# Cross attention on one core: nine batches instead of eight turned by VectorE, in groups of two and one, and ScalarE asking for the context's plain copies

## The chip, the cores and the metric

The kernel runs on one core of a Trainium2 chip. The metric is the device time of one execution in microseconds (us). Before the change the median of three runs was 129.13 us (129.09 to 129.58).

## What is computed

For each of 16 batches there are two inputs of 128 channels x 1024 positions, X (`x`) and G (`ctx_4096`), and eight 128x128 weights. Cut to what matters:

```python
def xca(q, k, v):                                   # 8 heads of 16 channels
    attn = softmax(einsum('bhni,bhnj->bhij', q, k) * scale, axis=-1)
    return einsum('bhnd,bhde->bhne', v, attn)       # back to [b, n, c]
res_p2r = xca(heads(rgb, wq_rgb), heads(geo, wk_point), heads(geo, wv_point)) @ proj_p2r.T
res_r2p = xca(heads(geo, wq_point), heads(rgb, wk_rgb), heads(rgb, wv_rgb)) @ proj_r2p.T
return transpose(rgb + res_p2r) + transpose(geo + res_r2p)
```

`rgb` is X and `geo` is G with channels last. The attention is over channels, so its scores are made of one 128x128 Gram matrix of X and G per batch, with the weights on both sides. For that Gram matrix (a sum over the 1024 positions) TensorE needs X and G with positions on the partitions, that is, turned.

## The kernel before, in words

The kernel is a hand-written pipeline over rounds. In round `i` the engines work on five batches at once: batch `i` is turned, batch `i-1` gets its Gram matrix (L291), batch `i-2` its products with the weights and its scores (uv, s), batch `i-3` its softmax and the two small products y (L342) and t (L355, L356), and batch `i-4` its output: twelve float32r matmuls of 512 columns from the plain copies (L312), split into a high and a low part. Round 16 is the last full one; a tail follows.

A batch can be turned in one of two ways.

- By TensorE (`on_tensor`): sixteen 128x128 transposes (L270) of the plain copies `x_raw`, `g_raw` into PSUM. ScalarE then copies X's half out (L438) and VectorE G's (L541).
- By VectorE (`on_vector`): four stream transposes of 32x32 blocks (L534) straight into `xt` and `gt`. They read `xz` and `gz`, a second copy of the batch, loaded by DMA in four parts of 32 partitions ("quads", L158), each with runs of 1 KB. A pair of batches fills one of two slots. The plain copy of the batch is loaded as well, for the output.

Before, the batches 5, 6, 8, 9, 11, 12, 14 and 15 are turned by VectorE.

All waits are written by hand on semaphores. Each engine runs its own list in order. These orders matter here:

- SyncE (its queue is SPq) asks in each round for plain copies of X and of G, 512 KB each, then for quads 0 and 1 of `xz` (X of a pair) or `gz` (G of a pair), then for a store. Before a plain copy into one of the six `x_raw`/`g_raw` slots it waits until GpSimd is done with the slot's last batch (`x_lo_ready`, `g_lo_ready`). Plain copies are asked for three rounds ahead of a batch that TensorE turns, one round ahead of one that VectorE turns.
- ScalarE (ACTq) asks for quads 2 and 3, one early and one late in its round, between its own copies.
- `issued_in` says in which round a pair is asked for: X in round 2, 4, then one round after the pair that used the slot before was turned; G one round after X. Before that `pair_turned` waits for the slot. The four quads of one tensor and pair add to one semaphore (`xz_loaded`, `gz_loaded`) and VectorE waits for all four.
- VectorE turns G's first half between the softmax's normalisation (L568) and its copy of y (L576), for which TensorE waits with the t product (L355).

Of the kernel before, what the change touches and what calls it, by code (L numbers as in the profile page):

```python
# [14 lines left out]
QUAD = 32  # L15
RAW_SLOTS = 6
SPLIT_SLOTS = 3
OUT_SLOTS = 5
PAIRS = 2
# [3 lines left out]
WQR, WKR, WKP, WQP, PP, PR, WVP, WVR = range(8)  # L23


VECTOR_PAIRS = ((5, 6), (8, 9), (11, 12), (14, 15))


def bass_cross_channel_attention(nc: bass.Bass, x, ctx, weights, out):
# [10 lines left out]
    B, C, N = x.shape  # L40
# [2 lines left out]
    HALF = N // 2  # L43
    TILES = N // TILE
    QUADS = P // QUAD
    on_vector = [b for pair in VECTOR_PAIRS for b in pair]
    on_tensor = [b for b in range(B) if b not in on_vector]
    assert C == P and HALF == BANK and B == 16 and on_tensor[0] == 0

    with ExitStack() as stack:  # L50
# [13 lines left out]
        x_raw = sb("x_raw", [P, RAW_SLOTS, N])  # L64
        g_raw = sb("g_raw", [P, RAW_SLOTS, N])
# [43 lines left out]
        x_loaded = [sem(f"x_loaded{s}") for s in range(RAW_SLOTS)]  # L109
        g_loaded = [sem(f"g_loaded{s}") for s in range(RAW_SLOTS)]  # L110
# [12 lines left out]
        xt_turned = sem("xt_turned")  # L123
        gt_ready = sem("gt_ready")
# [18 lines left out]
        x_lo_ready = sem("x_lo_ready")  # L143
        g_lo_ready = sem("g_lo_ready")
# [7 lines left out]

        def load_turned(eng, src, dst, loaded, pair, quads):

            first = VECTOR_PAIRS[pair][0]
            for q in quads:
                into = dst[q * QUAD:(q + 1) * QUAD, pair % PAIRS, :, :]
                eng.dma_start(into.rearrange("p e (a m) -> p (e a) m", a=QUADS),  # L158
                              src[q][:, QUADS * first:QUADS * (first + 2), :]).then_inc(loaded[pair % PAIRS], 16)

        def pair_turned(eng, pair):

            eng.wait_ge(xt_turned, 4 * pair + 4)
            eng.wait_ge(gt_ready, 2 * VECTOR_PAIRS[pair][1] + 2)

        def x_turned_half(eng, b, half):

# [2 lines left out]
            else:  # L170
                eng.wait_ge(xt_copied, 2 * on_tensor.index(b) + 1 + half)


        issued_in = {2 + 2 * pair if pair < PAIRS else VECTOR_PAIRS[pair - PAIRS][1] + 1: pair
                     for pair in range(len(VECTOR_PAIRS))}

        first, second = slice(0, HALF), slice(HALF, N)
        third, fourth = slice(HALF, HALF + HALF // 2), slice(HALF + HALF // 2, N)
# [31 lines left out]

        @block.sync
        def _(sp):
            def load_plain(b):
                slot = b % RAW_SLOTS
                sp.dma_start(x_raw[:, slot, :], x[b]).then_inc(x_loaded[slot], 16)
                sp.dma_start(g_raw[:, slot, :], ctx[b]).then_inc(g_loaded[slot], 16)

            def store(b):
                sp.wait_ge(half_copied, 2 * b + 2)
                sp.dma_start(out[b], out_sb[:, b % OUT_SLOTS, :]).then_inc(out_stored[b % OUT_SLOTS], 16)  # L220

            sp.dma_start(x_raw[:, 0, first], x[0][:, first]).then_inc(x_first, 16)
            sp.dma_start(x_raw[:, 0, second], x[0][:, second]).then_inc(x_loaded[0], 16)
            load_plain(1)
            sp.dma_start(w_sb[:, WQR:WKR + 1, :], weights[:, WQR:WKR + 1, :]).then_inc(wu_loaded, 16)
            load_plain(2)
            sp.dma_start(w_sb[:, WKP:, :], weights[:, WKP:, :]).then_inc(w_loaded, 16)
            load_plain(3)
            load_plain(4)

            for i in range(2, B + 4):
                for b in range(5, B):
                    if i == max(2, b - 1 if b in on_vector else b - 3):
                        if b >= RAW_SLOTS:
                            sp.wait_ge(x_lo_ready, b - RAW_SLOTS + 1)
                            sp.wait_ge(g_lo_ready, b - RAW_SLOTS + 1)
                        load_plain(b)
                x_pair, g_pair = issued_in.get(i), issued_in.get(i - 1)  # L240
                if x_pair is not None:
                    if x_pair >= PAIRS:
                        pair_turned(sp, x_pair - PAIRS)
                    load_turned(sp, x_turn, xz, xz_loaded, x_pair, (0, 1))
                if g_pair is not None:
                    load_turned(sp, g_turn, gz, gz_loaded, g_pair, (0, 1))
                if i >= 5:
                    store(i - 5)
            last_slot = (B - 1) % OUT_SLOTS
            sp.wait_ge(half_copied, 2 * B - 1)  # L250
            sp.dma_start(out[B - 1][:, first], out_sb[:, last_slot, first]).then_inc(last_stored[0], 16)
            sp.wait_ge(quarter_copied, 1)
            sp.dma_start(out[B - 1][:, third], out_sb[:, last_slot, third]).then_inc(last_stored[1], 16)
            sp.wait_ge(quarter_copied, 2)
            sp.dma_start(out[B - 1][:, fourth], out_sb[:, last_slot, fourth]).then_inc(last_stored[2], 16)
            for s in range(OUT_SLOTS):
                sp.wait_ge(out_stored[s], 16 * len(range(s, B - 1, OUT_SLOTS)))
            for part in range(3):
                sp.wait_ge(last_stored[part], 16)
# [157 lines left out]
        def _(act):  # L417
            def split_hi(b, raw, loaded, hi, hi_ready):
                plain_loaded(act, b, loaded)
                if b == 0:  # L420
                    act.wait_ge(x_first, 16)
                    act.wait_ge(g_first, 16)
                if b >= SPLIT_SLOTS:
                    act.wait_ge(half_done, 2 * (b - SPLIT_SLOTS) + 2)
                nc.scalar.copy(hi[:, b % SPLIT_SLOTS, :], raw[:, b % RAW_SLOTS, :]).then_inc(hi_ready, 1)  # L425

            def evacuate(b, half):
                act.wait_ge(half_done, 2 * b + 1 + half)
                if half == 0 and b >= OUT_SLOTS:
                    act.wait_ge(out_stored[b % OUT_SLOTS], 16 * (b // OUT_SLOTS))  # L430
                cols = slice(half * HALF, (half + 1) * HALF)
                nc.scalar.copy(out_sb[:, b % OUT_SLOTS, cols], out_ps[:, cols]).then_inc(half_copied, 1)  # L432
# [36 lines left out]
            for i in range(B + 1):  # L469
                s, y, l = i - 2, i - 3, i - 4  # L470
                x_pair, g_pair = issued_in.get(i), issued_in.get(i - 1)
                if s >= 0:
                    gram_high(s)
                if y >= 0:
                    exponents(y)
                if s >= 0:
                    split_hi(s, x_raw, x_loaded, x_hi, x_hi_ready)
                if x_pair is not None:
                    if x_pair >= PAIRS:
                        pair_turned(act, x_pair - PAIRS)  # L480
                    load_turned(act, x_turn, xz, xz_loaded, x_pair, (2,))
                if g_pair is not None:
                    load_turned(act, g_turn, gz, gz_loaded, g_pair, (2,))
                if l >= 0:
                    evacuate(l, 0)
                if l >= 0 and l != B - 4:
                    evacuate(l, 1)
                if s >= 0:
                    copy_uv(s)
                if i in on_tensor:  # L490
                    copy_xt(i, 0)
                if s >= 0:
                    split_hi(s, g_raw, g_loaded, g_hi, g_hi_ready)
                if x_pair is not None:
                    load_turned(act, x_turn, xz, xz_loaded, x_pair, (3,))
                if g_pair is not None:
                    load_turned(act, g_turn, gz, gz_loaded, g_pair, (3,))
                if i in on_tensor:
                    copy_xt(i, 1)
                if y >= 0:  # L500
                    t_high(y)
                if i == 1:
                    act.wait_ge(wu_loaded, 16)
                    nc.scalar.copy(wu_hi[:, :, :], w_sb[:, WQR:WKR + 1, :]).then_inc(wu_hi_ready, 1)
# [19 lines left out]
        @block.vector  # L524
        def _(dve):
            def turn_half(b, half, src, loaded, dst, turned):
                n = on_vector.index(b)
                pair, at = n // 2, n % 2
                dve.wait_ge(loaded[pair % PAIRS], 64 * (pair // PAIRS) + 64)
                dve.wait_ge(gram_done, b - 1)  # L530
                blocks = src[:, pair % PAIRS, at, :].rearrange("p (a j i) -> p j a i", a=QUADS, i=QUAD)
                first = half * TILES // 2
                cols = slice(half * HALF, (half + 1) * HALF)
                nc.vector.transpose(dst[:, b % 2, cols].rearrange("p (j a k) -> p j a k", a=QUADS, k=QUAD),  # L534
                                    blocks[:, first:first + TILES // 2, :, :]).then_inc(turned, 1)
# [119 lines left out]
```

## Time and profile before

| what | value |
|---|---|
| median of three runs | 129.13 us |
| profiled execution | 129.13 us, of which 127.1 us from its first to its last instruction |
| PE, ACT, POOL, DVE busy | 95%, 68%, 61%, 56% of the span |
| DMA moved | 34.25 MB, 270 GB/s over the span |
| x_raw, g_raw, median from issue to landing | 15.8 and 16.2 us |

PE is TensorE, ACT ScalarE, DVE VectorE, POOL GpSimd, SPq and ACTq the sequencers that issue DMAs. PEclk is the clock that TensorE was granted, in parts of full speed; it is 1.00 throughout. A time such as "at 63.8" is counted from the first instruction.

### The profile page before, as it was taken

The numbers are of one execution on the slowest core, as the hardware profiler recorded it, in microseconds if no ns is written. First come the engines' busy times: TensorE is split into PE (matmuls) and PEld (weight loads), VectorE is DVE, ScalarE is ACT, GpSimd is POOL, SyncE is SP. The second block draws the span as 40 slices with busy tenths as digits, with TensorE's granted clock in tenths as the row PEclk, the third lists the DMA queues.
The fourth block names the chain that finished last, engine by engine and source line by source line (L and its number), as shares of the span: only waits on it lengthen the run. The fifth ranks groups of instructions, "written<-read, shape, count | busy, mean of one in ns | idle before, by whom it ended". The sixth has DMA issues, their size and how long they took to land.

```text
span 127.1 us, 2678 instructions
## 1 busy us (share of the span) xinstructions
PE 120.8 (95%) x858; PEld 110.0 (87%) x858; DVE 71.4 (56%) x210; ACT 86.4 (68%) x195; POOL 77.3 (61%) x41
## 2 busy tenths in 40 slices
PE   6979999999999999999999999999999998997990
PEld 6859998899898989898989989999989897985880
DVE  0035364637878625969653787862596965546210
ACT  4133967875959595878787595959587868588351
POOL 5000779685495958195958559595819595937700
PEclk9999999999999999999999999999999999999999
DMA  3999999999999999999999999999999750003435
GB/s 102 362 398 409 419 285 252 230 289 256 296 243 251 246 328 370 328 271 281 313 274 339 380 328 282 278 280 300 329 418 419 317 233 1 0 23 147 168 142 191
DMA packets 16493, 34.25 MB, mean 270 GB/s; under 512 B 1376, under 2 KB 9952, under 8 KB 16480
## 3 DMA queue, kind: packets, MB, share of 16 engines
q1 hardware_dynamic: 11840, 29.36, 72.9%
q10 hardware_dynamic: 4640, 4.72, 14.4%
q8 instruction: 7, 0.11, 0.4%
q14 instruction: 6, 0.05, 0.1%
HBM read 25.69 MB, written 8.39 MB: 268 GB/s over the span
## 4 chain that ended last, share of the span: by engine, by line
PE 84%; DMA 5%; ACT 3%; issue 2%; DVE 1%; SPq 1%; ACTq 1%
PE out_ps L312 32%; PE gram_bank L291 21%; PE sy_bank L342 6%; DMA g_raw<-in_ctx_dram 5%; PE gt_ps L270 5%; PE xt_ps L270 4%; PE t_bank L355 3%; PE sy_bank L366 3%; PE sy_bank L365 3%; PE t_bank L356 3%; ACT expd L454 2%; PE uv_bank L333 1%; PE uv_bank L335 1%; PE uv_bank L334 1%; DVE probs L568 1%
## 5 line engine op out<-in xcount | busy, mean ns | idle before, releaser
L205 POOL TENSOR_TENSOR x_lo<-x_raw,x_hi 128x1024 fp32r<-128x1024 f32 x16 | 38.0, 2378 | 39.0 <-ACT x_hi L425 39.0
L208 POOL TENSOR_TENSOR g_lo<-g_raw,g_hi 128x1024 fp32r<-128x1024 f32 x16 | 38.0, 2373 | 2.5 <-ACT g_hi L425 2.5
L291 PE MATMUL gram_bank<-gt,xt 128*128 128x128 f32 x256 | 33.8, 275 | 0.0
L291 PEld LDWEIGHTS gram_bank<-gt,xt 128*128 128x128 f32 x256 | 31.2, 192 | 0.0
L541 DVE COPY gt<-gt_ps 128x512 f32<-128x512 f32 x16 | 11.0, 687 | 18.9 <-PE gt_ps L270 18.9
L432 ACT COPY out_sb<-out_ps 128x512 f32<-128x512 f32 x31 | 18.0, 581 | 5.2 <-PE out_ps L312 3.9
L454 ACT ACTIVATE expd<-scores,min_neg 128x128 f32<-128x128 f32 x32 | 12.6, 396 | 8.6 <-DVE min_neg L551 8.6
L425 ACT CAST g_hi<-g_raw 128x1024 fp32r<-128x1024 f32 x16 | 16.9, 1055 | 0.0
L425 ACT CAST x_hi<-x_raw 128x1024 fp32r<-128x1024 f32 x16 | 16.6, 1037 | 0.0
L438 ACT COPY xt<-xt_ps 128x512 f32<-128x512 f32 x16 | 9.4, 586 | 9.1 <-PE xt_ps L270 9.1
L312 PE MATMUL out_ps<-x_hi,t_hi 128*128 128x512 f32 x31 | 13.6, 440 | 0.0
L467 ACT CAST t_hi<-t_bank 128x256 fp32r<-128x256 f32 x16 | 5.9, 371 | 10.8 <-DVE t_bank L580 10.8
L312 PE MATMUL out_ps<-g_lo,t_hi 128*128 128x512 f32 x31 | 12.4, 402 | 0.0
L580 DVE TENSOR_TENSOR t_bank<-t_bank,ident 128x256 f32<-128x256 f32 x16 | 6.9, 432 | 9.6 <-PE t_bank L356 9.6
L312 PE MATMUL out_ps<-x_lo,t_hi 128*128 128x512 f32 x31 | 12.3, 397 | 0.0
L312 PE MATMUL out_ps<-g_hi,t_lo 128*128 128x512 f32 x31 | 12.2, 395 | 0.0
L312 PE MATMUL out_ps<-x_hi,t_lo 128*128 128x512 f32 x31 | 12.2, 395 | 0.0
L312 PE MATMUL out_ps<-g_hi,t_hi 128*128 128x512 f32 x31 | 12.2, 394 | 0.0
L576 DVE COPY y_sb<-sy_bank 128x256 f32<-128x256 f32 x16 | 6.8, 424 | 8.8 <-PE sy_bank L342 8.8
L534 DVE STREAM_TRANSPOSE gt<-gz 128x512 f32<-128x512 f32 x16 | 11.2, 702 | 0.0
L534 DVE STREAM_TRANSPOSE xt<-xz 128x512 f32<-128x512 f32 x16 | 11.0, 685 | 0.0
L342 PE MATMUL sy_bank<-w_sb,probs 128*128 128x128 f32 x64 | 9.9, 277 | 1.0 <-DVE probs L568 1.0
(80 smaller groups left out, 211.5 us busy)
## 6 DMA issues: line engine op xcount, KB each, us to landing
x_raw<-in_x_dram SPq DMA_DIRECT2D x15, 512.0 KB, 15.8
g_raw<-in_ctx_dram SPq DMA_DIRECT2D x15, 512.0 KB, 16.2
out_dram<-out_sb SPq DMA_DIRECT2D x15, 512.0 KB, 15.1
xz<-in_x_dram SPq DMA_DIRECT2D x8, 256.0 KB, 12.4
gz<-in_ctx_dram SPq DMA_DIRECT2D x8, 256.0 KB, 16.0
xz<-in_x_dram ACTq DMA_DIRECT2D x8, 256.0 KB, 11.8
gz<-in_ctx_dram ACTq DMA_DIRECT2D x8, 256.0 KB, 13.9
g_raw<-in_ctx_dram ACTq DMA_DIRECT2D x2, 256.0 KB, 4.6
```

The source lines that it names most:

```text
L205: nc.gpsimd.tensor_tensor(x_lo[:, slot, :], x_raw[:, raw_slot, :], x_hi[:, slot, :].bitcast(F32), ALU.subtract).then_inc(x_lo_ready, 1)
L208: nc.gpsimd.tensor_tensor(g_lo[:, slot, :], g_raw[:, raw_slot, :], g_hi[:, slot, :].bitcast(F32), ALU.subtract).then_inc(g_lo_ready, 1)
L270: last = nc.tensor.transpose(ps[:, t * TILE:(t + 1) * TILE], raw[:, b % RAW_SLOTS, cols], ident2[:, 0, :])
L291: last = nc.tensor.matmul(gram_ps, xt[:, b % 2, cols], gt[:, b % 2, cols], start=(t == 0), stop=(t == TILES - 1))
L312: last = nc.tensor.matmul(out_ps[:, cols], w[:, b % 2, which, :], moving[:, slot, cols], start=(n == 0), stop=(n == len(parts) - 1))
L342: last = nc.tensor.matmul(y_ps[:, a * P:(a + 1) * P], probs[:, a, :], w_sb[:, wv, :], start=True, stop=True)
L425: nc.scalar.copy(hi[:, b % SPLIT_SLOTS, :], raw[:, b % RAW_SLOTS, :]).then_inc(hi_ready, 1)
L432: nc.scalar.copy(out_sb[:, b % OUT_SLOTS, cols], out_ps[:, cols]).then_inc(half_copied, 1)
L438: nc.scalar.copy(xt[:, b % 2, half * HALF:(half + 1) * HALF], xt_ps[:, :]).then_inc(xt_copied, 1)
L454: nc.scalar.activation(expd[:, a, :], scores[:, a, :], ACT.Exp, bias=min_neg[:, a:a + 1], scale=-1.0, accum_out=row_sum[:, a:a + 1]).then_ ...
L534: nc.vector.transpose(dst[:, b % 2, cols].rearrange("p (j a k) -> p j a k", a=QUADS, k=QUAD), blocks[:, first:first + TILES // 2, :, :]).t ...
L541: nc.vector.tensor_copy(gt[:, b % 2, half * HALF:(half + 1) * HALF], gt_ps[:, :]).then_inc(gt_ready, 1)
```

## The change

VectorE turns nine batches: 5, 6, 8, 9, 10, 11, 13, 14 and 15, in the groups (5,6), (8,9), (10,11), (13,14) and (15). TensorE turns 0 to 4, 7 and 12. The slots for a group, the rounds in which it is asked for and its waits follow the same rule as before, so that group (10,11) is asked for in rounds 7 and 8, (13,14) in 10 and 11, and (15) in 12 and 13. From batch 5 on, the plain copies of G are asked for by ScalarE in the middle of its round, those of X by SyncE, each waiting only for the slot of its own tensor.

```diff
-VECTOR_PAIRS = ((5, 6), (8, 9), (11, 12), (14, 15))
+VECTOR_GROUPS = ((5, 6), (8, 9), (10, 11), (13, 14), (15,))
...
+            first, count = VECTOR_GROUPS[pair][0], len(VECTOR_GROUPS[pair])
             for q in quads:
-                into = dst[q * QUAD:(q + 1) * QUAD, pair % PAIRS, :, :]
+                into = dst[q * QUAD:(q + 1) * QUAD, pair % PAIRS, 0:count, :]
                 eng.dma_start(into.rearrange("p e (a m) -> p (e a) m", a=QUADS),
-                              src[q][:, QUADS * first:QUADS * (first + 2), :]).then_inc(loaded[pair % PAIRS], 16)
+                              src[q][:, QUADS * first:QUADS * (first + count), :]).then_inc(loaded[pair % PAIRS], 16)
...
-            eng.wait_ge(xt_turned, 4 * pair + 4)
-            eng.wait_ge(gt_ready, 2 * VECTOR_PAIRS[pair][1] + 2)
+            last = VECTOR_GROUPS[pair][-1]
+            eng.wait_ge(xt_turned, 2 * on_vector.index(last) + 2)
+            eng.wait_ge(gt_ready, 2 * last + 2)
...
+        def plain_issued_in(i):
+            return [b for b in range(5, B) if i == max(2, b - 1 if b in on_vector else b - 3)]
...
-        issued_in = {2 + 2 * pair if pair < PAIRS else VECTOR_PAIRS[pair - PAIRS][1] + 1: pair
-                     for pair in range(len(VECTOR_PAIRS))}
+        issued_in = {2 + 2 * pair if pair < PAIRS else VECTOR_GROUPS[pair - PAIRS][-1] + 1: pair
+                     for pair in range(len(VECTOR_GROUPS))}
...
+            def load_plain_x(b):
+                if b >= RAW_SLOTS:
+                    sp.wait_ge(x_lo_ready, b - RAW_SLOTS + 1)
+                sp.dma_start(x_raw[:, b % RAW_SLOTS, :], x[b]).then_inc(x_loaded[b % RAW_SLOTS], 16)
...
-                for b in range(5, B):
-                    if i == max(2, b - 1 if b in on_vector else b - 3):
-                        if b >= RAW_SLOTS:
-                            sp.wait_ge(x_lo_ready, b - RAW_SLOTS + 1)
-                            sp.wait_ge(g_lo_ready, b - RAW_SLOTS + 1)
-                        load_plain(b)
+                for b in plain_issued_in(i):
+                    load_plain_x(b)
...
+            def load_plain_g(b):
+                if b >= RAW_SLOTS:
+                    act.wait_ge(g_lo_ready, b - RAW_SLOTS + 1)
+                nc.scalar.dma_start(g_raw[:, b % RAW_SLOTS, :], ctx[b]).then_inc(g_loaded[b % RAW_SLOTS], 16)
...
                     split_hi(s, g_raw, g_loaded, g_hi, g_hi_ready)
+                for b in plain_issued_in(i):
+                    load_plain_g(b)
```

## Rows read from the trace of the kernel before

**Rows 1.** The page: busy shares, and the span in 40 equal slices.

```profile
PE 120.8 (95%) x858; PEld 110.0 (87%) x858; DVE 71.4 (56%) x210; ACT 86.4 (68%) x195; POOL 77.3 (61%) x41
...
DMA  3999999999999999999999999999999750003435
GB/s 102 362 398 409 419 285 252 230 289 256 296 243 251 246 328 370 328 271 281 313 274 339 380 328 282 278 280 300 329 418 419 317 233 1 0 23 147 168 142 191
```

**Rows 2.** The chain that ended last: start, us, what (rounds 9, 10, 13, 15).

```profile
57.78 2.81 PE out_ps L312 x12
...
62.28 0.22 PE t_bank L355 x2
...
64.06 2.81 PE out_ps L312 x12
...
67.23 0.44 PE xt_ps L270 x4
67.66 0.44 PE gt_ps L270 x4
...
72.10 2.81 PE out_ps L312 x12
...
84.66 2.81 PE out_ps L312 x12
...
98.97 2.81 PE out_ps L312 x12
```

**Rows 3.** Timeline of DVE in round 11: start, us, line, [idle before <-releaser].

```profile
73.99 0.70 DVE L534 STREAM_TRANSPOSE gt<-gz 128x512 f32<-128x512 f32 x1
74.61 0.67 DVE L534 STREAM_TRANSPOSE xt<-xz 128x512 f32<-128x512 f32 x1
75.74 0.42 DVE L576 COPY y_sb<-sy_bank 128x256 f32<-128x256 f32 x1 [0.45 <-PE sy_bank L342]
```

**Rows 4.** One issue of gz, the last ACTq one of batches 11, 12.

```profile
L158 ACTq DMA_DIRECT2D gz<-in_ctx_dram x1: 317/317/317, 54.8 to 54.8; - x1
...
DMA to landing us min/median/max: 17.0/17.0/17.0
```

**Rows 5.** The last SPq issue of gz, batches 14 and 15.

```profile
L158 SPq DMA_DIRECT2D gz<-in_ctx_dram x1: 2485/2485/2485, 77.1 to 77.1; - x1
...
DMA to landing us min/median/max: 16.3/16.3/16.3
```

**Rows 6.** Windows: stretch, its us, busy PE, PEld, DVE, ACT, POOL, PEclk, DMA, GB/s.

```profile
50.00:69.00 19.00, 19.00 (x133) 17.38 (x132) 13.36 (x39) 14.52 (x34) 12.87 (x6) 1.00 1.06 301
69.00:91.00 22.00, 22.00 (x160) 20.38 (x160) 14.21 (x41) 16.05 (x37) 15.26 (x7) 1.00 1.06 310
92.00:100.00 8.00, 8.00 (x56) 7.24 (x55) 6.73 (x22) 5.83 (x16) 4.97 (x3) 1.00 1.01 408
```

**Rows 7.** Timeline of SPq from 36 to 58 us.

```profile
44.37 0.33 SPq L215 DMA_DIRECT2D x_raw<-in_x_dram  x1
44.74 0.45 SPq L216 DMA_DIRECT2D g_raw<-in_ctx_dram  x1
...
52.41 4.69 SPq L158 DMA_DIRECT2D gz<-in_ctx_dram  x2
```

**Rows 8.** Waits of the SP queue: us in total, times, longest.

```profile
SPq L238 <- POOL g_lo L208: 13.4, 3, 7.6
```

**Rows 9.** Timeline of ACT in round 8, which issues two DMAs.

```profile
52.72 1.04 ACT L425 CAST x_hi<-x_raw 128x1024 fp32r<-128x1024 f32 x1
...
54.78 0.32 ACTq L158 DMA_DIRECT2D gz<-in_ctx_dram  x1
54.83 0.38 ACT L461 COPY uv<-uv_bank 128x256 f32<-128x256 f32 x1
```

**Rows 10.** Timeline: ACT in round 9 (no DMA), POOL's low part of batch 6.

```profile
59.00 1.03 ACT L425 CAST x_hi<-x_raw 128x1024 fp32r<-128x1024 f32 x1
...
56.23 2.38 POOL L208 TENSOR_TENSOR g_lo<-g_raw,g_hi 128x1024 fp32r<-128x1024 f32 x1
```

**Rows 11.** One ACTq issue of xz, ten us after ACTq's issue before it.

```profile
L158 ACTq DMA_DIRECT2D xz<-in_x_dram x1: 317/317/317, 64.8 to 64.8; - x1
...
DMA to landing us min/median/max: 9.0/9.0/9.0
```

More of the change, by code:

```diff
@@ L45, in bass_cross_channel_attention @@
     QUADS = P // QUAD
-    on_vector = [b for pair in VECTOR_PAIRS for b in pair]
+    on_vector = [b for group in VECTOR_GROUPS for b in group]
     on_tensor = [b for b in range(B) if b not in on_vector]
@@ L153, in load_turned @@
         def load_turned(eng, src, dst, loaded, pair, quads):
-            first = VECTOR_PAIRS[pair][0]
+            first, count = VECTOR_GROUPS[pair][0], len(VECTOR_GROUPS[pair])
             for q in quads:
-                into = dst[q * QUAD:(q + 1) * QUAD, pair % PAIRS, :, :]
+                into = dst[q * QUAD:(q + 1) * QUAD, pair % PAIRS, 0:count, :]
                 eng.dma_start(into.rearrange("p e (a m) -> p (e a) m", a=QUADS),
-                              src[q][:, QUADS * first:QUADS * (first + 2), :]).then_inc(loaded[pair % PAIRS], 16)
+                              src[q][:, QUADS * first:QUADS * (first + count), :]).then_inc(loaded[pair % PAIRS], 16)
         def pair_turned(eng, pair):
-            eng.wait_ge(xt_turned, 4 * pair + 4)
-            eng.wait_ge(gt_ready, 2 * VECTOR_PAIRS[pair][1] + 2)
+            last = VECTOR_GROUPS[pair][-1]
+            eng.wait_ge(xt_turned, 2 * on_vector.index(last) + 2)
+            eng.wait_ge(gt_ready, 2 * last + 2)
         def x_turned_half(eng, b, half):
@@ L212, in _ @@
         def _(sp):
+            def load_plain_x(b):
+                if b >= RAW_SLOTS:
+                    sp.wait_ge(x_lo_ready, b - RAW_SLOTS + 1)
+                sp.dma_start(x_raw[:, b % RAW_SLOTS, :], x[b]).then_inc(x_loaded[b % RAW_SLOTS], 16)
             def load_plain(b):
-                slot = b % RAW_SLOTS
-                sp.dma_start(x_raw[:, slot, :], x[b]).then_inc(x_loaded[slot], 16)
-                sp.dma_start(g_raw[:, slot, :], ctx[b]).then_inc(g_loaded[slot], 16)
+                load_plain_x(b)
+                sp.dma_start(g_raw[:, b, :], ctx[b]).then_inc(g_loaded[b], 16)
             def store(b):
@@ L233, in _ @@
             for i in range(2, B + 4):
-                for b in range(5, B):
-                    if i == max(2, b - 1 if b in on_vector else b - 3):
-                        if b >= RAW_SLOTS:
-                            sp.wait_ge(x_lo_ready, b - RAW_SLOTS + 1)
-                            sp.wait_ge(g_lo_ready, b - RAW_SLOTS + 1)
-                        load_plain(b)
+                for b in plain_issued_in(i):
+                    load_plain_x(b)
                 x_pair, g_pair = issued_in.get(i), issued_in.get(i - 1)
@@ L526, in turn_half @@
             def turn_half(b, half, src, loaded, dst, turned):
-                n = on_vector.index(b)
-                pair, at = n // 2, n % 2
+                pair = [b in group for group in VECTOR_GROUPS].index(True)
+                at = VECTOR_GROUPS[pair].index(b)
                 dve.wait_ge(loaded[pair % PAIRS], 64 * (pair // PAIRS) + 64)
```

## The prediction

> **What bounds the kernel now.** I read the page first. TensorE is busy 95% of the span, and in the line of slices the DMA engines stand at 9 as well until about slice 31, some 102 us, after which they are almost idle [rows 1]. So two things run full at once: TensorE, and until 102 us the DMA engines. Next I read the chain of work that ended last. Rounds start with the twelve output products. Round 9 starts at 57.78, round 10 at 64.06, round 11 at 72.10: a round without TensorE's turning takes 6.28 us, one with it 8.04 us. The difference is 16 transposes, in four rows of 0.44 us [rows 2]. Between the rows of a middle round nothing waits, so TensorE sets the pace, and DMA has so far been just in time. How just, the landings tell. The last part of gz for batches 11 and 12 landed at 54.8 + 17.0 = 71.8 us [rows 4]; VectorE began with it at 73.99 [rows 3]. For batches 14 and 15 it landed at 77.1 + 16.3 = 93.4 [rows 5]; round 14 starts one TensorE round after 84.66 [rows 2], at 92.7, so VectorE used it near 94.6. The slack is 2.2 and 1.2 us. In the windows the DMA share is 1.06 (the count is of overlapping packets, so it passes 1) at only 301 and 310 GB/s; once the turned loads are through, 408 GB/s [rows 6].
>
> **The change, part by part.**
>
> *TensorE.* One batch fewer is turned: 16 transposes, 8.04 - 6.28 = 1.76 us of a queue that is full, so this much is saved if everything arrives. The copies out of PSUM that go with it (ACT, DVE) lie beside it.
>
> *VectorE.* It gets four stream transposes of about 0.69 us for one batch, and loses two copies of the same length. That batches 8 to 11 stand in a row adds nothing: a VectorE-turned round shows DVE with a gap of 0.45 us before its copy of y [rows 3], so it fits in 6.28 us with no debt carried over. I take 0; if that gap is gone, each such round would be longer by what exceeds it, and nothing points to that.
>
> *When things are needed.* Round 10 still starts at 64.06, but rounds 11, 12 and 13 become 70.34, 76.62 and 84.66 (batch 12 is TensorE's now), 14 and 15 become 90.94 and 97.22. VectorE starts on gz 1.89 us into a round (73.99 - 72.10) [rows 2, 3]. How late may it be? After it come 0.67 and 0.42 us, then TensorE's t product, 4.50 us into the round (62.28 - 57.78) [rows 2]. From 1.89 with 0.70 + 0.67 + 0.42 one gets to 3.7, so about 0.8 us can be lost. The limit for gz is 2.7 us into the round: 66.8 for group (10,11), 87.4 for (13,14), 99.9 for (15).
>
> *When things land.* The DMA engines are full, so an earlier request gains nothing by itself; what counts is the bytes ahead. Ahead of the third group, the same four turned batches' and stores' bytes are queued as before, but not the plain X and G of batch 10, which are now asked for in round 9: 2 x 0.524 MB = 1.05 MB, at 301 GB/s [rows 6] 3.5 us. The group lands at 71.8 - 3.5 = 68.3: 1.5 us late. Ahead of the fourth, the plain copies of batch 13 are missing in the same way: 1.05 MB at 310 GB/s is 3.4 us, so it lands at 93.4 - 3.4 = 90.0, 2.6 us late. Behind it come two stores, X and G of 13 and of 14 (six times 0.524 MB) and group (15), 1.05 MB: 4.2 MB at 310 GB/s, 13.5 us, so 103.5: 3.6 us late. These delays aren't added up. A stall moves all later limits, so the total is the largest, 3.6 us. At 408 GB/s for the six plain ones (7.7 us) and 301 for the rest (3.5 us) the last term would be 11.2 and the delay 1.3; then the 2.6 of the group before it decides. I take 3.6, since quads are in the mix throughout, with 2.6 as the near bound.
>
> *G's plain copies on ScalarE.* For the bytes it changes nothing. What it does is reorder. SyncE waited 13.4 us in three places for GpSimd's g_lo [rows 8], one of them just before the plain copies of batch 10 at 44.37, with the xz and gz of the third pair behind them, the latter at 52.41 [rows 7]. These waits go, and SyncE's quads of gz are asked for some 5 to 8 us sooner. On ScalarE's queue two plain copies (8 and 9) now lie ahead of or between its own quads of the third group. Such a plain copy there isn't in the trace. Below, it takes 0.524 MB at 408 GB/s, 1.3 us; above, at half of 301 GB/s, 3.5 us: 2.6 to 7 us for the two, within work that is counted already. If both queues end together it costs 0; if ScalarE's ends last, while SyncE's goes on with later stores and X's, up to about half of 7 us. I take 0, nearer to a balanced pair of queues, since an ACTq quad was landed after 9.0 us [rows 11] where SPq's large copies need 16: ScalarE's queue is the quicker one. The bound of 3.5 us stays in the range. The Trainium skill (DMA: Bandwidth & Descriptors, Issuing engines are not separate DMA queues) says that DMAs started by different engines run on the same 16 DMA engines and only the time to initiate them is saved; the share of 1.06 with two queues open agrees, and by that rule this half of the change is worth nothing.
>
> *ScalarE's own time.* It issues 11 plain copies and four more quads, 0.32 us each [rows 9]. The issue at 54.78 lies under work of the engine: x_hi starts 1.2 us into round 9 without any issue [rows 10] as it does in round 8 with one before it (52.72, a round that starts at 51.5) [rows 9]. I take 0; without cover three issues in a round are 1 us. The new wait on g_lo has behind it, in ScalarE's list, the second quad, the copy of xt and t_hi, for which TensorE waits. For batch 12, in round 9, it asks for POOL's low part of G of batch 6, which ended at 56.23 + 2.38 = 58.6 [rows 10]; ScalarE comes to it near 62. Cost 0; it would cost only if POOL fell 3.5 us behind.
>
> *The sum*, against the profiled execution, 129.13 us (the median of the runs too): -1.76 + 3.6 = +1.8, so **131.0 us**. With 2.6 it is 130.0; with the ACT queue's 3.5 us on top, 134.5.
>
> **The rivals.**
>
> *A. All arrives in time: 127.4 us.* 129.13 - 1.76 = 127.4. For it: SyncE asks for the third group's quads 5 to 8 us sooner, and if the time from issue to landing kept at 16 us they would land near 63, before 66.8. Also, the rate is no constant: 408 GB/s was reached without quads [rows 6], and a luckier mix of the two queues would do. It decides when the mean rate up to 88 us is some 4% higher (3.6 of 90 us). Against it: the engines never ran dry [rows 1], so the 16 us are queueing, and a shorter queue ahead is what I have counted. Chance 0.28.
>
> *B. The stall just eats the gain: 128.5 to 129.8 us.* It needs a delay of 1.1 to 2.4 us, which is my third group's 1.5 alone, with the later ones made good by the 408 GB/s. Chance 0.15.
>
> *C. ScalarE's queue becomes the late one: 132.5 to 134.5 us.* G's plain copies, four for rounds 8 and 9 (8, 9, 10, 12), fill it, its quads of groups (10,11) and (13,14) end last, and later X's and stores go past them on SyncE's queue. The price is 1.5 to 3.5 us more. It decides if a plain copy on ACTq takes more than some 2.5 us of that queue. For it: VectorE waits for the slower of the two. Against it: rows 11's 9.0 us. The Trainium skill (DMA: Bandwidth & Descriptors, Queues, rings and completion order) states that each DMA engine goes round-robin between queues by packets. By it a queue of 4 KB packets gets more bytes than it had with 1 KB ones, which would speak for balance; no row here shows it. Chance 0.20.
>
> **How the numbers follow.** My forecast (129.8 to 132.5, at 131.0) has 0.37, A 0.28, B 0.15, C 0.20. About 0.5%, 0.65 us, is what a measurement here can tell from no change. Faster by more: A, 0.28, and a little of B's edge, 0.30. Within: the rest of B, 0.13. Slower: 0.57. The range must leave out no more than 2 in 10, and both signs hold much, so it goes from A's 127.3 to 133.6, inside C. The forecast's own range is 129.8 to 132.5.
>
> **What would show it.** In the profile after: rounds without turning at 6.28 us, seven with it; a hole in TensorE's row in round 10, 13 or 15, with VectorE idle before its transposes of gz or xz in those rounds, released by DMA; gz of the third group landing near 68, of the fourth near 90, of the last near 103. DMA at 9 in every slice to about 105 us, near 300 GB/s. ScalarE's x_hi still 1.2 us into its rounds. I am wrong if gz lands before 66.8 and 87.4 (A), which the GB/s between 50 and 90 us would explain, if they are above 310; or if ACTq's plain copies take much longer to land than 9 us, with TensorE waiting over 4 us (C).

## The result: 0.7% faster, against a forecast of 1.4% slower

The changed kernel took 128.12 us (median of 20 runs, 127.52 to 129.36), the kernel before 129.18 us (20 runs, 128.96 to 129.58) in the same sessions: ratio 0.993, 95% interval 0.991 to 0.995. The forecast was 131.0 us with 0.57 for slower; the time lies in its range (127.3 to 133.6) but on the other side of no change. Note the spread: 1.8 us, where the kernel before has 0.6. A ratio leaves out runs far above a kernel's fastest, so where an experiment below has such runs its times are listed. The profiled execution was one of the long ones, 129.34 us with a span of 127.1 us, as long as that of before, so its profile shows the whole gain and what ate it.

The page of the changed kernel, the parts that answer to [rows 1]:

```profile
PE 119.6 (94%) x842; PEld 108.8 (86%) x842; DVE 72.6 (57%) x212; ACT 85.2 (67%) x193; POOL 77.3 (61%) x41
...
PE   6979999999999999999996899999999998997991
...
GB/s 101 359 396 416 419 298 262 236 210 298 309 292 251 358 408 235 338 309 312 382 329 419 298 285 346 398 319 368 305 384 327 306 170 0 0 8 165 168 121 209
...
q1 hardware_dynamic: 10832, 24.12, 57.3%
q10 hardware_dynamic: 6800, 11.01, 29.3%
```

TensorE has 16 instructions fewer and 1.2 us less busy time, and one dip to 6, at about 68 us. q1 is SyncE's DMA queue, q10 ScalarE's, which has 6.3 MB more than before (4.72 MB and 14.4%): eleven copies of G, 5.8 MB, and the quads of the ninth batch. The chain of work that ended last, in order of time (start, us, what), and the waits:

```profile
51.64 2.82 PE out_ps L316 x12
...
55.30 13.27 DMA gz<-in_ctx_dram
...
70.26 0.49 PE t_bank L359 x2
...
72.31 2.80 PE out_ps L316 x12
...
78.59 2.81 PE out_ps L316 x12
...
86.62 2.80 PE out_ps L316 x12
...
92.90 2.81 PE out_ps L316 x12
...
99.18 2.81 PE out_ps L316 x12
```

```profile
DVE gt L545 <- DMA gz<-in_ctx_dram: 2.4, 1, 2.4
...
PE t_bank L359 <- DVE y_sb L587: 1.6, 1, 1.6
```

From the start of round 8 to that of round 11 there are three rounds in which TensorE turns nothing, 3 x 6.28 = 18.84 us; from 51.64 to 72.31 they took 20.67. So there is one hole of 1.8 us, in round 10, and it is the only wait of VectorE for a turned load. The last quad of gz of batches 10 and 11 was asked for by ScalarE at 55.3 and landed at 68.6, and VectorE's list shows it, with the t product waiting behind:

```profile
65.75 0.42 DVE L579 TENSOR_TENSOR probs<-expd,row_inv 128x256 f32<-128x256 f32 x1
68.59 0.71 DVE L545 STREAM_TRANSPOSE gt<-gz 128x512 f32<-128x512 f32 x1 [2.42 <-DMA gz<-in_ctx_dram]
69.23 0.67 DVE L545 STREAM_TRANSPOSE xt<-xz 128x512 f32<-128x512 f32 x1
```

Behind it the rounds are 6.28 and 8.03 us long again; group (13,14) landed at 75.6 + 9.6 = 85.2 and (15) at 90.3 + 9.0 = 99.3, neither late. The windows, to set beside [rows 6] (stretch, its us, busy PE, PEld, DVE, ACT, POOL, PEclk, DMA, GB/s):

```profile
50.00:69.00 19.00, 18.69 (x128) 16.88 (x126) 13.67 (x40) 14.27 (x34) 13.05 (x7) 1.00 1.06 342
69.00:86.00 17.00, 15.74 (x114) 14.66 (x115) 10.80 (x31) 10.81 (x25) 11.56 (x5) 1.00 1.06 333
```

The DMA share is the same 1.06 as before, but the rate is 342 GB/s where it was 301. Over 69 to 86 us it was 312 before. A single window depends on which loads fall into it; over the first 88 us the rate is 319 against 300. The columns are the same, and the first line is the kernel before:

```profile
0.00:88.00 88.00, 85.69 (x624) 78.75 (x625) 51.23 (x148) 61.17 (x137) 54.59 (x32) 1.00 1.03 300
0.00:88.00 88.00, 84.29 (x612) 77.70 (x613) 51.24 (x148) 59.30 (x134) 53.67 (x31) 1.00 1.03 319
```

Which queue was late? [rows 4] give the landing of the third group, 71.8 us, with the ScalarE issue at 54.8, because the four quads share one semaphore and the landings are matched to the issues in order. The packets say otherwise. Between 65.0 and 68.5 us the kernel before had none on q10 (the first line below: queue, packets, MB, share of 16 engines), so ScalarE's quads were through and the group waited for SyncE's, asked for at 52.4 [rows 7]. In the changed kernel (the other two lines, the same stretch) SyncE asked for its quads of gz at 44.0, they had landed by 60.2, and the last quad was ScalarE's. The late queue has changed sides.

```profile
q1 hardware_dynamic: 521, 0.94, 106.4%
...
q1 hardware_dynamic: 203, 0.73, 58.0%
q10 hardware_dynamic: 208, 0.56, 43.5%
```

### The profile page after: what moved, and what is told of

The parts are those of the page before. It is cut to its first block, busy times and chain, and to the rows that moved or that the text cites. A ratio compares the mean times of both kernels' runs of the same rounds, so it can differ in the third digit from the quotient of the medians.

```text
span 127.1 us, 2642 instructions
## 1 busy us (share of the span) xinstructions
PE 119.6 (94%) x842; PEld 108.8 (86%) x842; DVE 72.6 (57%) x212; ACT 85.2 (67%) x193; POOL 77.3 (61%) x41
## 4 chain that ended last, share of the span: by engine, by line
PE 71%; DMA 16%; ACT 3%; issue 3%; DVE 2%; SPq 1%; ACTq 1%; DVEq 0%
PE out_ps L316 28%; PE gram_bank L295 18%; DMA gz<-in_ctx_dram 10%; DMA g_raw<-in_ctx_dram 5%; PE sy_bank L346 5%; PE gt_ps L274 4%; PE xt_ps L274 4%; PE t_bank L359 3%; PE sy_bank L370 2%; PE t_bank L360 2%; PE sy_bank L369 2%; ACT expd L463 2%; PE uv_bank L337 1%; PE uv_bank L339 1%; PE uv_bank L338 1%
## 5 line engine op out<-in xcount | busy, mean ns | idle before, releaser
L552 DVE COPY gt<-gt_ps 128x512 f32<-128x512 f32 x14 | 9.6, 688 | 17.0 <-PE gt_ps L274 17.0
L476 ACT CAST t_hi<-t_bank 128x256 fp32r<-128x256 f32 x16 | 5.9, 372 | 12.7 <-DVE t_bank L591 12.7
L545 DVE STREAM_TRANSPOSE gt<-gz 128x512 f32<-128x512 f32 x18 | 12.6, 702 | 2.4 <-DMA gz<-in_ctx_dram 2.4
L447 ACT COPY xt<-xt_ps 128x512 f32<-128x512 f32 x14 | 8.2, 587 | 8.5 <-PE xt_ps L274 8.5
L545 DVE STREAM_TRANSPOSE xt<-xz 128x512 f32<-128x512 f32 x18 | 12.3, 685 | 0.0
## 6 DMA issues: line engine op xcount, KB each, us to landing
xz<-in_x_dram ACTq DMA_DIRECT2D x8, 256.0 KB, 12.7
```

What stands on the lines that cost most here:

```text
L447: nc.scalar.copy(xt[:, b % 2, half * HALF:(half + 1) * HALF], xt_ps[:, :]).then_inc(xt_copied, 1)
L552: nc.vector.tensor_copy(gt[:, b % 2, half * HALF:(half + 1) * HALF], gt_ps[:, :]).then_inc(gt_ready, 1)
```

## The experiments

The first set asked where this rate comes from and what the hole in round 10 hangs on. "The change" is the changed kernel.

**G's copies back on SyncE (g_on_sync).** The new groups, the old way of asking:

```diff
                 for b in plain_issued_in(i):
-                    load_plain_x(b)
+                    if b >= RAW_SLOTS:
+                        sp.wait_ge(x_lo_ready, b - RAW_SLOTS + 1)
+                        sp.wait_ge(g_lo_ready, b - RAW_SLOTS + 1)
+                    sp.dma_start(x_raw[:, b % RAW_SLOTS, :], x[b]).then_inc(x_loaded[b % RAW_SLOTS], 16)
+                    sp.dma_start(g_raw[:, b % RAW_SLOTS, :], ctx[b]).then_inc(g_loaded[b % RAW_SLOTS], 16)
...
-                for b in plain_issued_in(i):
-                    load_plain_g(b)
```

> The new groups, but G's plain copies asked for by SyncE again, with its waits on x_lo and g_lo. Theory 1 (the split of the plain copies over two queues raises the rate of the DMA engines): between 50 and 86 us the rate falls back from 333 to 342 GB/s to about 300 to 312, the last gz of batches 10 and 11 lands at 70 or later, that of 13 and 14 near 90, and the time is 130 to 131.5 us. Theory 2 (the rate rose because more turned bytes or another order of groups mix better, whoever asks for G): rate, landings and time as with the change, 128.1 us.

Measured: runs of 127.40, 127.78, 128.69, 129.03, 132.87 and 134.38 us. In the profiled one (129.03) the rate was 313 and 329 GB/s in the two windows; the gz of (10,11) landed at 67.7, that of (13,14) at 89.1 and (15) at 99.6. The landing at 89.1 is what theory 1 and my forecast (90.0) had; 67.7 is near the forecast 68.3 but short of theory 1's 70, and the time was no clear 130. ScalarE's queue had only 10 packets between 65.0 and 68.5 us, so the late quads were SyncE's, as before the change. The two long runs had a mean granted clock of 0.974 and 0.987; to this I come back.

**The old groups with G on ScalarE (old_groups_g_on_act).** `VECTOR_GROUPS = ((5, 6), (8, 9), (11, 12), (14, 15))` in the changed kernel.

> The old eight batches in their old pairs, with G's plain copies asked for by ScalarE. Both theories expect no gain in time, since TensorE had no wait for DMA in the middle: 129.1 us, within 0.3%. Theory 1: the rate between 50 and 86 us rises from 301 to 312 to 320 or more, and the last gz of batches 11 and 12 lands 3 us or more before 71.8. Theory 2: the rate stays near 305 and the landing near 71.

Measured: 128.99 us, ratio 0.9985 (0.9976 to 0.9993). The rate between 50 and 69 us was 333 GB/s against 301, and 315 between 69 and 86. The last gz of (11,12) landed at 55.3 + 12.8 = 68.1, not 71.8. Same bytes, same rounds, so this goes to theory 1: asked for over two queues, the same loads are through 3.6 us sooner. The edit also shortens SyncE's list and its waits, which this run can't tell from the split itself.

**ScalarE's quad ahead of G (quad_before_g, and again).**

```diff
-                for b in plain_issued_in(i):
-                    load_plain_g(b)
                 if x_pair is not None:
                     load_turned(act, x_turn, xz, xz_loaded, x_pair, (3,))
                 if g_pair is not None:
                     load_turned(act, g_turn, gz, gz_loaded, g_pair, (3,))
+                for b in plain_issued_in(i):
+                    load_plain_g(b)
```

> The changed kernel, with ScalarE's second quad asked for before G's plain copies in the same round, not behind them. If the 1.9 us hole in round 10 comes from ScalarE's queue, whose last quad of gz stands behind G of batch 9, that quad lands about 2 us sooner, near 66.5, and the time is 127.4 to 127.7 us with little scatter. If it is the bytes in both queues that count, the landing stays near 68.5 and the time at 128.1.

> ScalarE's second quad ahead of G, beside the changed kernel on one chip. If the order in ScalarE's queue decides when the third group is whole, all runs lie at 127.4 to 128.0 us here too, whatever the changed kernel does.

> The changed kernel itself, as the control on the chip of this call. On the first chip it took 127.5 to 129.4 us. The two kernels of the last call that should have been as fast had a hole of 5 to 6 us in round 10 and took 133 us and more, with TensorE's granted clock down to half for some us behind the hole. If that was their chip, the changed kernel can do the same here: a part of its runs at 132 to 134 us. If it was their edit, it stays within 129.4.

Measured: 127.42 us, ratio 0.987 (0.9853 to 0.9886), and in the second session 127.47 (0.9854 to 0.988) beside 127.83 for the change on that chip, whose runs went up to 128.77. The landing of the last quad, one row of each in that session, first the change, then this:

```profile
L158 ACTq DMA_DIRECT2D gz<-in_ctx_dram x1: 456/456/456, 55.3 to 55.3; - x1
...
DMA to landing us min/median/max: 12.7/12.7/12.7
```

```profile
L158 ACTq DMA_DIRECT2D gz<-in_ctx_dram x1: 317/317/317, 54.8 to 54.8; - x1
...
DMA to landing us min/median/max: 9.1/9.1/9.1
```

68.0 against 63.9 (65.0 in the first session), with the limit at 66.8, and no wait of VectorE for a turned load is left. So the hole is one of order in ScalarE's queue: G of batch 9, not needed before round 11, stood ahead of a quad needed in round 10. The edit gained 4.1 us of landing time, more than the 1.3 to 3.5 us that I had given one such copy. The rate between 50 and 69 us rose too, to 361 GB/s, with the same requests on the same two queues.

**Seven slots (g_on_sync_7_slots, quad_before_g_7_slots).** `RAW_SLOTS = 7` in g_on_sync and in quad_before_g.

> As g_on_sync, but with seven slots for the plain copies, so that SyncE waits for GpSimd's low parts one batch less. If SyncE's waits were what held the loads back, this comes near the change, 128.1 us, with the rate near 340 GB/s; if the two queues are what counts, it stays within 0.5 us of g_on_sync.

> The version with ScalarE's second quad ahead of G, with seven slots for the plain copies. All theories expect that nothing is late any more: 127.1 to 127.4 us, as TensorE alone allows, and no gain beyond that.

Measured: 127.24 us (ratio 0.9844, 0.9831 to 0.9856; four runs of 127.1 to 127.4 and one of 133.3), and 127.46 us (0.9847, 0.9814 to 0.9879), all five within 0.1. In the first, SyncE waited 2.3 us for GpSimd's g_lo instead of 10.7, the group landed at 66.2 and the rate was 333 GB/s, with G on SyncE. So the waits for the slots were a part of the late landing too; theory 1 alone isn't the story.

**Quad 2 on SyncE as well (quad2_on_sync, and again).** `(0, 1, 2)` in both `load_turned` calls of SyncE, and ScalarE's two calls with `(2,)` gone.

> The changed kernel, with quad 2 of every group asked for by SyncE as well, so that ScalarE has one quad beside each plain copy of G. In the changed kernel SyncE's quads of gz of batches 10 and 11 land by 60.2 and ScalarE's last at 68.6. If the longer of the two queues is what makes it late, the group lands 2 us or more sooner, and the time is 127.4 to 127.7 us. If the bytes are what counts, it lands near 68.5 and the time stays at 128.1.

> Quad 2 on SyncE as well, beside the changed kernel on one chip. If the longer queue decides, 127.4 us; if G of batch 9 ahead of ScalarE's last quad is what makes it late (the edit leaves that as it was), it is no better than the changed kernel.

Measured: 129.17 to 134.50 us in six runs; again, beside the change, 127.42 to 130.62, median 129.85. A shorter queue on ScalarE didn't help: in the second session the group landed at 55.3 + 12.7 = 68.0, as in the change, and the rate from 50 to 69 us was 299 GB/s. The idea that moving a quad off ScalarE's queue is enough fell; G of batch 9 still stood ahead of the one that was left, and SyncE's list was longer.

**Two stores less (no_stores_2_3, and again).** The stores of batches 2 and 3 are left out, with the waits on them.

> The changed kernel without the stores of the batches 2 and 3 (left out), 1.05 MB less in SyncE's queue ahead of and beside the third group's loads. If every byte in either queue delays the group, it lands about 3 us sooner (1.05 MB at 342 GB/s), the hole in round 10 is gone, and the time is 127.4 us. If only ScalarE's own queue counts, the landing stays above 67.5 and the time near 128.1.

> The changed kernel without the stores of the batches 2 and 3 (left out), beside the changed kernel on one chip. In the runs of DMAs alone, four stores beside one-sided quads took 291 GB/s and four loads beside them 239. If what lies beside the quads counts more than the bytes, this is as late as the changed kernel or later, though it moves 1.05 MB less: 128.5 us or more. If bytes count, 127.4.

Measured: 129.64 to 134.15 us, and in the session of the change's 127.83, 129.73 to 131.91 (ratio to the kernel before 1.013, 1.008 to 1.017). 1.05 MB less, and slower: the last quad landed at 55.2 + 14.6 = 69.8. The rate was 298 GB/s from 50 to 69 us, where the change on that chip had 330. The bytes ahead of a load don't tell when it lands, then; my sum was built on that. The edit isn't bytes alone, though: with the two stores gone SyncE asks for X of batch 11 at 45.8 us instead of 48.3, so another load lies beside ScalarE's quads.

**DMAs alone.** Two kernels without computation (all of it is left out), whose phases are told in the expectations.

> No computation: only DMAs in nine phases, one behind the other, with both queues empty in between. 4 or 8 copies of 512 KB (plain) and 8 or 16 turned quads of 256 KB. Phase 1: eight plain on SyncE. 2: eight quads (0, 1) on SyncE. 3: quads 0, 1 on SyncE beside quads 2, 3 on ScalarE. 4: four plain on SyncE beside quads 2, 3 on ScalarE. 5: four stores beside quads 2, 3. 6: four plain and eight quads in turn on SyncE alone. 7: four plain on each. 8: X, G, quad 0, quad 1 in turn on SyncE beside quads 2, 3 on ScalarE (the split before). 9: X, quads 0, 1 on SyncE beside quad 2, G, quad 3 on ScalarE (the split of the change), the same bytes as phase 8. Theory 1 (the split itself raises the rate): phase 9 takes 5 to 10% less than phase 8, and a phase with its two queues level is faster than one whose SyncE queue has much more. Theory 2 (the split is worth nothing; the rate in the kernel depends on what falls together with what): 8 and 9 agree within 2%, and the phases with quads on one side of the partitions alone, 2 and 4, are the slow ones.

> DMAs alone again, seven phases with both queues empty in between. 1: the split before (a store, X, G, quads 0 and 1 in turn on SyncE, four times, beside quads 2 and 3 on ScalarE). 2: the split of the change (G between quads 2 and 3 on ScalarE), the same bytes. 3: as 2 with G behind quad 3. 4 and 5: as 1 and 2, but ScalarE starts only when half of SyncE's list has landed, so that SyncE's queue is alone for a part. 6: stores and G on SyncE beside quads 2, 3. 7: X and G beside them. If the split is worth nothing, 1, 2 and 3 agree within 2%. If what costs is that one queue stands empty while the other holds quads of one side of the partitions, 4 takes 8% or more longer than 1 and 5 likewise. If a load beside one-sided quads is dearer than a store, 7 takes 10% or more longer than 6.

Each phase is a window below (for these kernels: stretch, its us, busy POOL, PEclk, DMA share, GB/s). Of dma_alone phases 2 (quads 0, 1 on one queue), 3 (quads on both), 4 (loads beside one-sided quads), 5 (stores beside them), 6 (one queue with everything), 8 (the split before) and 9 (the split of the change):

```profile
15.40:26.60 11.20, 0.00 (x0) 1.00 0.95 187
...
28.60:43.40 14.80, 0.00 (x0) 1.00 1.06 283
...
45.10:62.70 17.60, 0.00 (x0) 1.00 1.00 238
...
64.40:78.80 14.40, 0.00 (x0) 1.00 1.03 291
...
80.60:103.00 22.40, 0.00 (x0) 1.00 0.97 186
...
117.00:146.00 29.00, 0.00 (x0) 1.00 1.02 289
148.00:177.50 29.50, 0.00 (x0) 1.00 1.01 284
```

Of dma_streams all seven:

```profile
9.00:40.90 31.90, 0.00 (x0) 1.00 1.05 328
42.60:74.30 31.70, 0.00 (x0) 1.00 1.04 330
76.10:108.00 31.90, 0.00 (x0) 1.00 1.03 328
109.40:146.60 37.20, 0.00 (x0) 1.00 1.03 282
148.10:185.70 37.60, 0.00 (x0) 1.00 1.02 278
187.50:209.60 22.10, 0.00 (x0) 1.00 0.99 283
211.40:234.10 22.70, 0.00 (x0) 1.00 1.00 277
```

The first three windows are the split before, the split of the change, and G behind the quads: 31.9, 31.7 and 31.9 us. Phases 8 and 9 of the first kernel, the same test without stores, took 29.0 and 29.5 us. With both queues full the split is worth nothing.

The fourth and fifth carry the same bytes, with ScalarE's queue held back until half of SyncE's list has landed: 37.2 and 37.6 us, 16 to 19% longer. Not all of that is lost while ScalarE's queue is empty, as parts of the phases show (first phase, twice the fourth):

```profile
9.00:28.60 19.60, 0.00 (x0) 1.00 1.05 324
...
109.40:129.00 19.60, 0.00 (x0) 1.00 1.05 308
...
141.50:145.50 4.00, 0.00 (x0) 1.00 1.02 186
```

With SyncE's queue alone the rate is 308 GB/s where the first phase had 324 (in the fifth phase 304 over its first 15.9 us, where the second had 342). The rest is lost at the end, when SyncE's list is through and ScalarE's quads are left alone, at 186 GB/s.

Quads of one side of the partitions alone on one queue run at 187 GB/s, and one queue with plain copies and quads in turn at 186, although in all of these the DMA share reads 0.95 to 1.06. So the share says that the engines have packets in hand, not that they move them at full rate. The last two windows (stores and loads beside quads, and loads alone) are 283 and 277 GB/s: the 10% that I expected between a store and a load isn't there when they come mixed, though phases 4 and 5 of the first kernel differ by 22%. Whether a store is cheaper beside a quad stays open.

Phase 4 also shows what the prediction had no row for. From 51 to 54 us SyncE's plain copies (4 KB packets) ran beside ScalarE's quads (1 KB packets):

```profile
q1 hardware_dynamic: 212, 0.78, 81.2%
q10 hardware_dynamic: 211, 0.20, 22.5%
```

The two queues moved the same number of packets and very unequal bytes, 0.78 and 0.20 MB. A quad beside plain copies on the other queue gets a fifth of the bytes.

**A hole made on purpose (hole_2, hole_5).** In the kernel before, four or eight extra stream transposes into a spare tile ahead of VectorE's first gz of round 11; the work is added, nothing is left out:

```diff
+                if i == 11:
+                    for n in range(4):                      # 8 in hole_5
+                        nc.vector.transpose(scratch[:, n, :]..., xz[:, 0, 0, :]...)
                 if i in on_vector:
                     turn_half(i, 0, gz, gz_loaded, gt, gt_ready)
```

> The kernel before, with four stream transposes of 0.70 us into a spare tile ahead of VectorE's first gz of round 11 (added work): 2.8 us, of which 0.8 are slack, so a hole of 2.0 us in TensorE. Theory 1 (a hole costs its length): 131.2 us. Theory 2 (a long enough hole also lowers TensorE's granted clock, a short one does not): 131.2 as well, with the clock at 1.00.

> The same with eight transposes: 5.6 us, less 0.8 slack, a hole of 4.8 us. Theory 1: 134.0 us with the clock at 1.00. Theory 2: the clock is granted at 0.5 for some us behind the hole, which costs 1 to 3 us more: 135 to 137 us, mean clock 0.97 to 0.99.

Measured: hole_2 130.97 us (ratio 1.012), clock 1.00 in all four runs. hole_5 135.35 us (ratio 1.047, 1.041 to 1.053), clock 0.974 to 0.987 in all four. The forecast by length, 134.0, took 0.70 us for a transpose. In the profiles the four took 2.48 us together and the eight 4.86, so with the 0.8 us of slack the holes are 1.7 and 4.1 us. hole_2 paid 1.7 (130.97 against 129.28), just its length; hole_5 paid 6.1, 2.0 more than its own. The windows of hole_5's profiled run (136.74 us), its longest, columns as in [rows 6]:

```profile
76.00:78.00 2.00, 1.25 (x12) 1.06 (x10) 2.00 (x4) 1.41 (x3) 2.00 (x2) 1.00 1.07 288
78.00:80.00 2.00, 0.00 (x0) 0.00 (x0) 2.00 (x4) 0.00 (x0) 1.85 (x1) 1.00 1.08 241
80.00:82.00 2.00, 0.95 (x4) 0.95 (x5) 1.61 (x4) 0.00 (x0) 0.00 (x0) 0.61 1.08 291
82.00:84.00 2.00, 2.00 (x12) 2.00 (x11) 0.86 (x2) 0.37 (x1) 0.00 (x0) 0.50 1.10 344
84.00:86.00 2.00, 2.00 (x8) 1.71 (x8) 1.13 (x6) 1.00 (x5) 0.00 (x0) 0.50 1.03 314
86.00:88.00 2.00, 2.00 (x8) 1.56 (x7) 1.97 (x5) 1.65 (x4) 0.78 (x1) 0.68 1.09 237
88.00:90.00 2.00, 2.00 (x17) 1.87 (x16) 0.39 (x3) 1.19 (x4) 1.61 (x1) 1.00 1.06 271
```

TensorE stands still from about 77.3 to 81 us (1.25 us busy of the two before 78, 0.95 of the two before 82), and is then granted 0.50 of its 2.4 GHz, that is the 1.2 GHz level, until about 87 us. The hole is paid once more behind it, in part. So it is with the long runs of g_on_sync, quad2_on_sync and no_stores_2_3: those of 131.3 us and more have mean clocks of 0.974 to 0.987 too, all but one (132.15 us at 1.00, not profiled), and in the profiled ones the clock falls right behind a longer wait in round 10. The shortest of these standstills is 2.9 us (no_stores_2_3 again, and g_on_sync in the next set).

**Change and g_on_sync in one session (g_on_sync_again, change_third, g_on_sync_third).**

> The new groups with G's plain copies on SyncE, a second time on whatever chip, since its six runs lay at 127.4 to 129.0 and at 132.9 and 134.4 us. If the two long ones were a hole of over 4 us with the clock down behind it, such runs show a mean clock under 0.99 here too, and the others 1.00; the changed kernel, in 26 runs, never passed 129.4.

> The changed kernel in one call with the kernel that differs from it only in who asks for G's plain copies. If ScalarE's queue, kept filled by them, is worth the 16% that an empty one cost in the runs of DMAs alone, for the part of the time in which it would be empty, this one is the faster of the two by 0.5 us or more: 127.5 to 128.5 us.

> The new groups with G's plain copies on SyncE, beside the changed kernel in one call. If a filled ScalarE queue matters: 0.5 to 4 us slower than the changed kernel, 128.5 to 132.5 us, and a rate between 50 and 69 us at least 15 GB/s below. If the split is worth nothing in the kernel either: the same within 0.3 us.

Measured: g_on_sync again 130.57 to 133.82 us (six runs). In one session, the change 127.98 us (127.68 to 128.68), all at clock 1.00; g_on_sync 127.22, 127.32, 129.66, 131.72, 131.76 and 131.96, the last three at 0.984 to 0.987. The windows from 50 to 69 us, first the change, then g_on_sync:

```profile
50.00:69.00 19.00, 18.45 (x127) 16.64 (x125) 14.97 (x43) 14.23 (x33) 13.05 (x7) 1.00 1.06 331
```

```profile
50.00:69.00 19.00, 18.68 (x128) 16.86 (x126) 13.27 (x39) 14.25 (x34) 13.04 (x7) 1.00 1.07 280
```

In its profiled run, 131.96 us, VectorE waited 3.8 us for the group, which was whole at 69.9. ScalarE's queue had 14 packets from 65.0 to 68.5 us and SyncE's 398, so it waited for SyncE's quads. So the kernel with G on SyncE can be as fast as any (127.2), and is the less steady of the two by far.

## Why the prediction was wrong, point by point

- **TensorE's term, -1.76 us, was right.** Rounds are 6.28 and 8.03 us, and with the hole gone quad_before_g took 127.4, which is what rival A's sum gave.
- **The limits were right.** I had 66.8 us for the third group; it landed at 68.6 and the hole was 1.8 us. In quad_before_g 63.9 left none.
- **The third group's landing was near by luck.** Forecast 68.3, measured 68.6 in the profile (68.0 in another session). I had it from all bytes ahead, in both queues, at 301 GB/s, starting from a landing that I put down to ScalarE's queue and that was SyncE's. The bytes moved at 342 GB/s, SyncE's quads came much sooner, and ScalarE's last quad was kept back by G of batch 9 ahead of it. Two errors cancelled: the rate, and the 0 that I took for the order in that queue.
- **The step that failed is "these delays ... the total is the largest, 3.6 us".** The later landings were 85.2 and 99.3, not 90.0 and 103.5, since I had taken 310 GB/s from the kernel before as a property of full DMA engines. It isn't: with G on SyncE the fourth group did land at 89.1. At 319 instead of 300 GB/s some 1.7 MB more had moved by 88 us, which at the forecast's 310 is 5.4 us, about what the landings gained (4.8 and 4.2). So the term of +3.6 us was worth nothing. Only the hole of the third group was left, 1.8 us in the profiled run and, by the distance from 127.4, some 0.7 in the median and 0.1 in the best. That is -1.76 + 0.7 = -1.1 us.
- **"For the bytes it changes nothing. ... this half of the change is worth nothing" was wrong in the kernel.** From 50 to 69 us the rate was higher by 32 GB/s with the old groups, and with the new ones by 51 in one session. DMAs alone agree with the rule that I cited there from the Trainium skill (DMA: Bandwidth & Descriptors, Issuing engines are not separate DMA queues) as long as both queues are full: 31.9 and 31.7 us, 29.0 and 29.5. They don't when one queue runs dry: the same bytes then took 16 to 19% longer. In the kernel before, ScalarE asks for nothing from 34 to 44 and from 55 to 65 us, but its queue ran dry only behind that, from about 65 to 68.5 in the second case, and by the 5 to 11% that a dry ScalarE queue cost there, 3.5 us of it are worth 0.4 us at most. What raised the rate in the kernel is not shown. Three edits raised it, and no run isolates what they have in common: G on ScalarE, shorter waits of SyncE (seven slots, 313 to 333 GB/s from 50 to 69 us), and the swap in ScalarE's list (361).
- **Rival A** named its condition, a mean rate up to 88 us over 4% higher; it was 6% (319 against 300), and A came true but for the one hole. **Rival B**, the third group's stall alone with the later ones made good, is what happened, and the nearest to the median; eight of the 20 runs lie in its 128.5 to 129.8. **Rival C** had the right place (ScalarE's queue ends last, SyncE's quads of the group had landed by 60.2) and the wrong size, and a tail worse than I knew: behind a hole as long as hole_5's the clock falls.
- ScalarE's and VectorE's own time: nothing seen, as forecast.

## What to carry to other kernels

A busy share of DMA near 1 is not a rate limit: before you price a landing by bytes over GB/s, look what each queue held in that stretch, for engines with a share of 0.95 to 1.06 moved anything from 186 to 361 GB/s. When several loads add to one semaphore, find the queue that was late from its packets, and not from the last issue; before the change it was SyncE's, after it ScalarE's. Order the loads in a queue by when they are needed; here one swap of two lines (quad before G) took the hole away: 127.5 us beside the change's 127.8 in one session (its 20 runs have 128.1), with 0.4 us of scatter instead of 1.3. A long hole in TensorE costs more than its length, because of the lowered clock behind it, so a margin of 2 us in the landings is worth more than it looks.

## What the hardware showed that was not expected

- Turned quads on one queue alone: 187 GB/s; on both queues, opposite sides of the partitions: 283. Plain copies and quads in turn on one queue: 186 GB/s, 22.4 us; the same bytes on two queues (phase 4): 238 GB/s, 17.6 us.
- With 4 KB packets on one queue and 1 KB packets on the other, both moved the same number of packets (212 and 211 in 3 us).
- Standstills of TensorE of 1.4 us (hole_2) and 1.6 us (the change) left the granted clock at 1.00. Behind those of 2.9 us it was 0.50 for some 3 us, and behind the 3.8 us of hole_5 for about 6 us; there the kernel paid 6.1 us (135.35 against 129.28) for 4.1 us of hole.
- Leaving out 1.05 MB of stores made the third group's last quad land 1.8 us later than in the change on the same chip (69.8 against 68.0). No run explains this.
